# Attention loop: values of two steps in one block, maxima over two banks, and six of sixteen probability tiles summed by accumulating DMAs

## What is computed

```
tp = silu(time_emb) @ Wt + bt                 # six vectors of 512 a batch
h = layernorm(x, g1, be1) * (1 + scale_msa) + shift_msa
h = attention(h)                              # 16 heads of 32
x = x + gate_msa * h
h = layernorm(x, g2, be2) * (1 + scale_mlp) + shift_mlp
x = x + gate_mlp * (gelu(h @ W1 + b1) @ W2 + b2)

def attention(h):
    q, k, v = split(h @ Wqkv + bqkv)
    attn = softmax(q @ k.T * 32 ** -0.5)      # 2048 x 2048 for each batch and head
    return (attn @ v) @ Wproj + bproj
```

## Time and profile before

| | us |
|---|---|
| median of three runs | 3696.48 |
| span of the profiled execution | 3696.8 |
| PE busy | 3452.4 |
| DVE busy | 2266.1 |
| POOL busy | 1775.8 |
| ACT busy | 1552.4 |
| maxima reductions, DVE L1147 (2048) | 1267.9 |
| exponentials, ACT L1104 (2048) | 1080.4 |
| additions, POOL L1083 (320) | 1474.1 |
| products for maxima, PE L1213 (2048) | 855.1 |
| score products, PE L1261 (2048) | 868.8 |
| value products, PE L1228 (4096) | 548.7 |

### The profile page before, as it was taken

One profiled execution on the slowest core, in us unless ns is written; L12 is line 12 of the kernel. 1 busy time (PEld: TensorE's weight loads), 2 busy tenths in 40 slices (PEclk: granted clock), 3 DMA queues, 4 the chain that ended last, 5 costly groups with the idle time before them and its releaser, 6 DMA issues. The chain is left out here.

```text
span 3696.8 us, 51173 instructions
## 1 busy us (share of the span) xinstructions
PE 3452.4 (93%) x17516; PEld 2197.3 (59%) x17516; DVE 2266.1 (61%) x3547; ACT 1552.4 (42%) x2751; POOL 1775.8 (48%) x527
## 2 busy tenths in 40 slices
PE   7899996997999999999999999999995779999999
PEld 6488885775544444444444444444434658888887
DVE  1378874444978788788788887887715932222222
ACT  0111114341166666666656666666662242222222
POOL 1033321001288788787887887877885500000000
PEclk9999998997699999999999999999997889999999
DMA  4122224446201222102222022200004641111100
GB/s 163 66 93 88 91 80 172 172 158 183 46 17 34 43 47 44 38 16 44 47 48 44 7 44 47 47 10 13 7 6 154 216 146 68 40 40 40 37 32 23
DMA packets 158137, 250.59 MB, mean 68 GB/s; under 512 B 46939, under 2 KB 68699, under 8 KB 151774
## 3 DMA queue, kind: packets, MB, share of 16 engines
q1 hardware_dynamic: 147166, 230.96, 21.1%
q10 hardware_dynamic: 10752, 16.79, 1.5%
HBM read 158.89 MB, written 88.08 MB: 67 GB/s over the span
## 5 line engine op out<-in xcount | busy, mean ns | idle before, releaser
L1147 DVE TENSOR_REDUCE att_mx<-att_pM 128x1 f32<-128x512 f32 x2048 | 1267.9, 680 | 336.2 <-PE att_pM L1213 334.0
L1104 ACT ACTIVATE att_prob<-att_pS 128x512 f32<-128x512 f32 x2048 | 1080.4, 601 | 772.8 <-PE att_pS L1261 765.2
L1083 POOL TENSOR_TENSOR att_acc<-att_acc,att_prob 128x2048 f32<-128x2048 f32 x288 | 1327.5, 4609 | 129.2 <-ACT att_prob L1104 104.1
L1213 PE MATMUL att_pM<-att_ks,att_qs 96*128 96x512 f32 x2048 | 855.1, 432 | 54.7 <-DVE att_mx L1147 33.6
L1261 PE MATMUL att_pS<-att_qs,att_ks 98*128 98x512 f32 x2048 | 868.8, 430 | 10.2 <-ACT att_prob L1104 8.0
L1261 PEld LDWEIGHTS att_pS<-att_qs,att_ks 98*128 98x128 f32 x2048 | 386.2, 190 | 555.1 <-ACT att_prob L1104 385.7
L1228 PE MATMUL att_pO<-att_prob,att_V 128*32 128x512 f32 x4096 | 548.7, 608 | 0.7 <-ACT att_prob L1104 0.7
L1213 PEld LDWEIGHTS att_pM<-att_ks,att_qs 96*128 96x128 f32 x2048 | 405.4, 198 | 200.5 <-DVE att_mx L1147 120.3
L1627 DVE TENSOR_TENSOR mlp_us<-mlp_tu,mlp_us 128x512 fp32r<-128x512 f32 x128 | 89.7, 700 | 536.0 <-ACT mlp_us L1600 536.0
L1670 PE MATMUL mlp_pu<-mlp_hs,mlp_W 128*128 128x512 f32 x1536 | 370.7, 391 | 18.9 <-DVE mlp_W L1619 18.9
L1689 PE MATMUL mlp_pa<-mlp_W,mlp_us 128*128 128x512 f32 x1536 | 368.8, 389 | 0.0
(11 more groups left out here) (181 smaller groups left out, 2984.7 us busy)
## 6 DMA issues: line engine op xcount, KB each, us to landing
qk_d<-qkv_qs SPq DMA_DIRECT2D x64, 512.0 KB, 2.7
att_qs<-qk_d SPq DMA_DIRECT2D x48, 512.0 KB, 7.4
att_ks<-qk_d SPq DMA_DIRECT2D x48, 512.0 KB, 13.8
gat_xT<-in_xT SPq DMA_DIRECT2D x32, 256.0 KB, 3.1
gat_xrow<-in_x SPq DMA_DIRECT2D x32, 256.0 KB, 2.8
x_d<-gat_x SPq DMA_DIRECT2D x32, 256.0 KB, 2.1
qkv_xr<-x_d SPq DMA_DIRECT2D x8, 1024.0 KB, 5.8
v_d<-qkv_vs SPq DMA_DIRECT2D x32, 256.0 KB, 2.0
```

What stands on the lines that cost most here:

```text
L1083: nc.gpsimd.tensor_tensor(acc[half][:], old[:], new[:], ALU.add).then_inc(added, 1)
L1104: nc.scalar.activation(prob[step % PR][:, c, :], pS[n % 3][:], ACT.Exp, scale=SCALE).then_inc(exp_done, 1)
L1147: nc.vector.tensor_reduce(mx[:, n // 4, n % 4:n % 4 + 1], bank(g, n)[:], AX.X, ALU.max).then_inc(m_read, 1)
L1213: nc.tensor.matmul(bank(g, n)[:], qs[k][0:KD, h, t * P:(t + 1) * P], ks[k][0:KD, h, mc * 512:(mc + 1) * 512], start=True, stop=True).then_ ...
```

## The change

The attention phase is rewritten in five respects.

**Values in blocks of two steps.** `behind(g, p)` makes the value products of steps 2p and 2p + 1 one after the other, once in two steps (after the third score product of every even step). ACT is told by `pair_done`, once for both. There are eight `prob` buffers instead of four.

**Maxima over two banks.** `pM` is two tiles of two banks each. Two products (i = 0, 1) fill one, and one reduction of 128 x 2 x 512 takes both. A group has 64 reductions instead of 128. `pS` has two banks instead of three. A table, `place`, numbers the fillings of `pM` in PE's order.

**Sums.** `ADDED` is now 0, 1, 3, 5, 7, 9, 11, 13, 14, 15: nine additions on POOL. The tiles of `SENT` (2, 4, 6, 8, 10, 12) are summed in an SBUF tile `gathered`: SP copies tile 2 into it (`send_first`), and POOL issues DMAs with `accum_op=ALU.add` for the other five (`send`), each after the one before has landed. `finish` sums `gathered` and `acc`, at the fifth step of the next half, behind the value block.

**End of a half.** The multiplication of `oc` by `rec` moves from DVE to POOL (`scale`, after the fourth addition of the next half); the reciprocals stand at steps 6 to 9; the stores move from ACT to SP.

**Groups.** All 16 are written out, and queries and keys have three buffers instead of four.

```diff
-        U = 4
-        PR = 4
-        ADDED = [0, 1, 2, 4, 5, 6, 8, 9, 11, 12, 13]
+        U = 3
+        PR = 8
+        SENT = [2, 4, 6, 8, 10, 12]
+        ADDED = [t for t in range(MT) if t not in SENT]
...
-        pS = [m.ps(f"pS{i}") for i in range(3)]
-        pM = [m.ps(f"pM{i}") for i in range(3)]
+        pS = [m.ps(f"pS{i}") for i in range(2)]
+        pM = [m.ps(f"pM{i}", [P, 2, 512]) for i in range(2)]
...
+            def send_first(n):
+                step = n % 2 * MT + SENT[0]
+                sp.wait_ge(exp_done, (n // 2 * ST + step) * 4 + 4)
+                if n >= 1:
+                    sp.wait_ge(z_done, n)
+                sp.dma_start(gathered[:], prob[step % PR][:]).then_inc(first_sent, 16)
...
+            for g in range(NG):
+                if g >= 1:
+                    sp.wait_ge(pair_done, g * ST // 2)
+                    if g + 2 < NG:
+                        load(g + 2)
+                    if g + 1 < NG:
+                        load_v(g + 1)
+                    send_first(2 * g)
+                    store(2 * g - 1)
+                else:
+                    send_first(0)
+                send_first(2 * g + 1)
+                if g + 1 < NG:
+                    rows(g + 1)
+                store(2 * g)
...
+            def send(n, j):
+                step = n % 2 * MT + SENT[j]
+                pool.wait_ge(exp_done, (n // 2 * ST + step) * 4 + 4)
+                if j == 1:
+                    pool.wait_ge(first_sent, (n + 1) * 16)
+                else:
+                    pool.wait_ge(sent, (n * (len(SENT) - 1) + j - 1) * 16)
+                nc.gpsimd.dma_start(gathered[:], prob[step % PR][:], accum_op=ALU.add).then_inc(sent, 16)
...
                         nc.gpsimd.tensor_tensor(acc[half][:], old[:], new[:], ALU.add).then_inc(added, 1)
+                        if ADDED[i] - 1 in SENT[1:]:
+                            send(n, SENT.index(ADDED[i] - 1))
+                        if i == SCALED and n >= 1:
+                            pool.wait_ge(added, n * NA + i)
+                            scale(n - 1)
...
-                nc.vector.tensor_reduce(mx[:, n // 4, n % 4:n % 4 + 1], bank(g, n)[:], AX.X, ALU.max).then_inc(m_read, 1)
+                nc.vector.tensor_reduce(mx[:, q // 2, q % 2:q % 2 + 1], bank(at)[:], AX.XY, ALU.max).then_inc(m_read, 1)
...
+            def behind(g, p):
+                for step in (2 * p, 2 * p + 1):
+                    last = values(g, step)
+                last.then_inc(pair_done, 1)
+
+            def finish(n):
+                if n:
+                    pe.wait_ge(z_read, n)
+                pe.wait_ge(sent, (n + 1) * (len(SENT) - 1) * 16)
+                sums(gathered, True, False)
                 pe.wait_ge(added, (n + 1) * NA)
+                sums(acc[n % 2], False, True).then_inc(z_done, 1)
+
+            def scores(g, step, c):
+                at = (g * ST + step) * 4 + c
...
+                if at >= 2:
+                    pe.wait_ge(exp_done, at - 1)
+                nc.tensor.matmul(pS[at % 2][:], ks[k][:, h, mt * P:(mt + 1) * P], qs[k][:, h, lc * 512:(lc + 1) * 512],
+                                 start=True, stop=True).then_inc(s_done, 1)
+                pair = m_pair(g, step, c // 2)
+                if pair:
+                    maxima(*pair, c % 2)
...
+                    for c in range(4):
+                        scores(g, step, c)
+                        if step % 2 == 0 and c == 2 and (g or step):
+                            before = g * ST // 2 + step // 2 - 1
+                            behind(before // (ST // 2), before % (ST // 2))
+                            if step % MT == 2 * FINISH and (g or step >= MT):
+                                finish(2 * g + step // MT - 1)
```

More of the change, by code:

```diff
@@ L980, in attention_phase, with m_pair @@
         o_v = io["o_d"].rearrange("(g h p) (b n) -> g h p b n", h=2, p=HD, b=B)
[L982 removed]
+        def m_pair(g, step, half):
             ahead = 1 if step < ST - LEAD else 2
[L986 to L995 removed]
@@ L997, in bank @@
[L997 to L1014, removed]
@@ L1016, in half_before, with fill @@
-        def half_before(g, step):
-            return 2 * g + step // MT - 1
+            return (g + ahead, (step + LEAD) % ST * 2 + half) if g + ahead < NG else None
+        place = {}
+        def fill(what):
+            place[what] = len(place)
+        for q in range(NQ):
+            fill((0, q))
+        for q in range(EARLY):
+            fill((1, q))
+        fill("turned 0")
+        for q in range(EARLY, LEAD * 2):
+            fill((1, q))
+        for g in range(NG):
+            for step in range(ST):
+                if step == ST - LEAD + 1 and g + 1 < NG:
+                    fill(f"turned {g + 1}")
+                for half in range(2):
+                    if m_pair(g, step, half):
+                        fill(m_pair(g, step, half))
@@ L1182, in _ @@
-            for n in range(EARLY):
-                maxima(1, n)
-            parts(0, 0)
-            for n in range(EARLY, LEAD * MS):
-                maxima(1, n)
-            def body(g, k, pair):
+            for q in range(NQ):
+                maxima(0, q)
+            top_of(0)
+            for q in range(EARLY):
+                maxima(1, q)
+            parts(0)
+            for q in range(EARLY, LEAD * 2):
+                maxima(1, q)
+            for g in range(NG):
                 for step in range(ST):
-                    if step == ST - LEAD and before(g, NG - 1):
+                    n = 2 * g + step // MT - 1
+                    if step == ST - LEAD and g + 1 < NG:
@@ L1200, in _ @@
-            groups(dve, body)
-            for c in range(5):
-                invert(2 * NG - 1, 1, NG - 1, c)
+                    if step == ST - LEAD + 1 and g + 1 < NG:
+                        parts(g + 1)
+                    for half in range(2):
+                        if m_pair(g, step, half):
+                            maxima(*m_pair(g, step, half))
+                    if 0 <= step % MT - INVERT < 4 and n >= 0:
+                        invert(n, step % MT - INVERT)
+            for c in range(4):
+                invert(2 * NG - 1, c)
```

306 lines of the change are left out of this document (137 added, 169 removed).

## The result

The changed kernel takes 3826.07 us (median of four runs, 3822.39 to 3834.05) against 3697.39 for the kernel before (median of four, taken beside it): ratio 1.0352, 95% interval 1.0331 to 1.0373, slower by 129 us. I had forecast slower by 39. The direction and the range held, the size didn't. The profiled execution spans 3821.2 us, 124.4 more than the one of before.

A forecast was written before the change was run, and what follows sets the result against it. PE, busy 93%, was taken as the bound. On 3696.8 us: 29.6 halves with maxima +36, 2.4 without +10, opening -5, unrolling -3, end +1, together +39, giving 3736 us; range 3650 to 3930.

The forecast's parts named there:

- The loads that share the engines: At each group's start, 3.5 MB of loads were to delay only the first, plain copy of the transfers, which stays hidden.
- L: Time from POOL's start of issuing an accumulating 1 MB transfer to its landing, taken as 7.5 us; the least certain number.
- My own sign for this case: Sign of a wrong forecast: POOL idle behind DMAs and PE idle before the gathered sums; right: no long wait for `gathered`.
- 2.4 halves without maxima: Halves at the phase's end: 52.5 us each by a score-chain cycle of 6.35 us a pair; +4 each, +10 us.
- PE's saving of 8.3 us eaten by the banks: PE's half without waits would be 48.2 us, 8.3 us less; not forecast because the edit takes PSUM banks away.
- Score chain, maxima chain: Two-bank waits between value blocks: two steps take 6.58 us by scores, 6.70 by maxima; halves +1.2 each, +36 us.
- the tops of the maxima: A term in the sum for one half with maxima: +0.2 us.
- Opening -5: Before the main part: 152 reductions of 0.599 us (91.0) become 76 of 1.13 (86), so -5 us.
- half clock as a rival: PE falling to the 1.2 GHz level; new waits of 0.15 to 0.9 us thought too short, longer only behind late transfers.
- Unrolling -3: Loops written out: one turn before showed PE idle 1.85 us and clock 0.73 over the next 5 us; -3 us.
- the loops: POOL's half, 5 x 4.7 + 4 L, and the transfers' 6 L + 5; they reach 57.7 us at L 8.6 and 8.8.
- transfers set the pace: Rival: accumulating transfers hold each half, 61 us at L 9.3, about 3845 us in all, or 4050 at 10.5; 31%.

The follow-up runs named there:

- run 2: Changed kernel without the six transfers per half and all waits for them, `gathered` holding ones (for timing alone): 3792.75 us, ratio 1.0254.
- run 1: Changed kernel with SP's loads held back until the last accumulation of the half before has landed: 3804.6 us, ratio 1.0292.
- run 6: Changed kernel with three single banks for scores and three for maxima, and without the six transfers per half: 3597.1 us, ratio 0.9729.
- run 12: Against run 10, two score banks and two pairs of maxima banks instead of three single banks each: 3875.07 us, ratio 1.0470.
- run 3: Changed kernel with three single banks for scores and three for maxima, reductions of 512 columns: 3771.08 us, ratio 1.0205.
- run 4: Changed kernel with eight unread 512-column products per two steps added in the last group: 3815.72 us, ratio 1.0322.
- run 14: Changed kernel with loads held back as in run 1 and the last group filled as in run 4: 3785.18 us, ratio 1.0235.
- run 10: Changed kernel with three single banks each for scores and maxima, one-step value blocks, no transfers, five tiles by ones-products: 3666.33 us, ratio 0.9909.
- run 5: Changed kernel with three single banks each for scores and maxima, and loads held back until the last accumulation has landed: 3774.2 us, ratio 1.0201.
- run 7: Against run 5, value blocks of one step instead of two: 3775.68 us, ratio 1.0206.
- run 8: Changed kernel with three single banks each, two-step value blocks kept, no transfers, five tiles by ones-products, eleven added by POOL: 3706.34 us, ratio 1.0021.
- run 11: Changed kernel with three single banks each, two-step blocks kept, three transfers per half instead of six, two tiles by ones-products: 3653.7 us, ratio 0.9874.

## Why the prediction was right and wrong

**The step that failed** is the sentence "The loads that share the engines [...] delay only the first, plain copy, which has until POOL's third addition." I took each half's transfers as a block that ends before the next loads start. But in the half shown above the five accumulations are issued 7.5, 9.5, 9.5 and 8.0 us apart, 34.5 us in all, where PE's cycles of two tiles take 6.7 to 7.8: after the second one POOL waits 2.8 us for a reciprocal, the third lands only after 9.0 us, the fourth after 7.4. So the fifth is issued when the next group's loads start. I had L nearly right (7.0 measured, 7.5 taken), but didn't lay the fifth one's issue time beside SP's `pair_done` wait. The transfers cost 41 us in the 29 halves (run 2), 28 of them by the loads (run 1). My own sign for this case was there: POOL waits 96.9 us in all for `gathered`, up to 4.2 at a time. The other large miss is the 2.4 halves without maxima, whose cycle I worked out at full clock.

Point by point:
- *PE's saving of 8.3 us eaten by the banks*: right. Runs 2 and 6 differ in the banks (and the place of the reciprocals): 58.07 against 53.09 per half. Even three banks don't give 48.2.
- *Score chain, maxima chain*: right in place and size. Each score product with two banks is 1.18 us behind the last but one (run 12); the plain cycle is 6.71 for 6.70, the one with a reciprocal 7.40 for 7.4, and every other half of run 2 takes 57.6 as forecast. The mis-sized term is the tops of the maxima, +0.2 a half: the halves in which they are made take 58.7, 1.1 us more, or 0.5 for each half. The measured half before is 56.63, so 57.6 alone would be +28 over 29 halves, and the tops bring it to +41; I had +33.
- *Opening -5*: wrong sign, +6. I counted chained reductions. In fact a pair of reductions comes every 2.54 us, with a hole of 0.18 in which DVE waits for PE, at PE's half clock (0.50); with three banks there is no hole. Rows of DVE's timeline after, and one of run 3, against the earlier trace rows:

```profile
908.95 2.35 DVE L1185 TENSOR_REDUCE att_mx<-att_pM 128x1 f32<-128x1024 f32 x2 [0.18 <-PE att_pM L1242]
911.49 2.36 DVE L1185 TENSOR_REDUCE att_mx<-att_pM 128x1 f32<-128x1024 f32 x2 [0.19 <-PE att_pM L1242]
```

```profile
901.74 76.62 DVE L1185 TENSOR_REDUCE att_mx<-att_pM 128x1 f32<-128x512 f32 x128 [20.90 <-PE att_pM L1241]
```

  1.27 us per 1024 columns, against 2 x 0.599 = 1.20 in single banks. The second of two starts 2.36 - 1.22 = 1.14 after the first: the chained figure was right, but every second reduction isn't chained.
- *2.4 halves without maxima, +10*: the largest miss after the transfers, +35.6 in the last three halves. My cycle of 6.35 stands in the trace for some 20 us (6.4 to 6.5) and then PE drops to the 1.2 GHz level. I had half clock as a rival, but only behind late transfers: the waits are short, so I thought them harmless. But without maxima PE has only eight products and a block per cycle, 1.9 + 2.3 = 4.2 us of work in 6.4, and in that stretch the granted clock fell (1.00 to 0.76). The kernel before kept 0.99 over its own such stretch, 2667 to 2785 us, where it has ones-products beside the scores and values. Runs 4 and 14 show the clock as a cause of the excess. The Trainium skill ("TensorE: Matmul & The Clock Gate", "Part 1: The HAM clock gate") calls half rate the default, which activity releases; the trace agrees, and I applied it only to the opening.
- *Unrolling -3*: not tried by itself. Among the halves of before three stand out, by 1.6 to 3.4 us; in run 10, unrolled, none does. Only the longest lies at a turn of PE's loop; for the two others I have no cause.
- *L and the loops*: L was right, and POOL's loop too in a half without loads (54.3 us in run 5 for 53.5). With the loads it was short: the mean half of runs 5 and 7 is 58.5. The Trainium skill ("DMA: Bandwidth & Descriptors", "Anatomy of one DMA") gives the estimates of 4.4 us for the copy and 6.8 for doubled data; the measured medians, 4.6 and 7.0, are close.
- *The rival "transfers set the pace"* is what happens with three banks (runs 5 and 7), at 54 to 58 us in the halves without loads and 59 to 63 in those with. With two banks it decides only in the halves with a collision.

Sum of the misses: transfers +41, last three halves +25, opening +11, regular halves +8, together 85; 39 + 85 = 124, the difference of the two profiled executions. Of the 41, 12.7 have no cause that a run shows.

## What to carry to other kernels

A chain of transfers that is hidden by its mean may still be late at one place: lay the last one of each round on the time axis beside the next burst on the same engines, and see whose buffer it holds. Where work is taken off the engine that sets the pace, cost the banks or buffers paid for it first; here two score and two pair banks cost about 200 us (runs 6 and 12), and the longer value blocks brought less than nothing (runs 8 and 11). And a stretch that loses its companion work needs its clock checked before its cycle is believed.

## What the runs showed of the hardware

- A DMA that adds 1 MB in SBUF to 1 MB in SBUF lands in 7.0 us (median of 160; the longest 16.6), a plain one in 4.6. Issuing it takes POOL 0.87 us. One after another they come every 7.5 us at best.
- An adding transfer issued 0.1 to 0.7 us behind the first of 3.5 MB of loads lands after 15.7 to 16.6 us, one issued 0.8 to 1.5 us ahead of them after 9.4 to 10.4 (13 places in the changed kernel's trace); it isn't served alongside them at its own rate.
- A maximum over 1024 columns in two banks follows the last one by 1.14 us at best (opening) and 1.19 in the plain cycle, two over 512 take 1.20: next to nothing is saved by the pair.
- Unread products in a thin stretch made it shorter (run 14: 30 us of them, 19 us less), with the granted clock at 0.97 instead of 0.75.
